# Row work of the last three stages of a graph network carried by the last 24 steps of their aggregations

## The chip, the cores and the metric

The kernel runs on 1 core of one Trainium2 chip (trn2). The metric is the time in microseconds that the device needs for one execution, as the median of several. SP, the engine without arithmetic here, issues transfers; ScalarE and GpSimd issue transfers too.

## The reference

Four layers of a graph network on 3125 nodes with 256 features and 50000 edges sorted by target node. Each layer adds its output to x; its input is relu(layernorm(x)). The first is two attention convolutions, the second adds tables, sigmoids and sums of edge attributes, the third is a convolution by relation and base, the fourth two hypergraph convolutions. What the change touches is the end of the third layer and the fourth:

```
# third: the kernel has the products with W ready in rel_d and gathers them
x = x + sum over edges of weight * (h[src] @ W[rel])
# fourth
h0 = relu((x - mean) / sqrt(var + 1e-5))                   # over features
def hconv(h, w1, b1, w2, b2, g, b):
    h = relu(h @ w1 + b1)
    agg = segment_sum(weight[:, None] * h[src], dst)
    return relu(bn(agg @ w2 + b2, g, b))                   # bn: over all nodes, with eps 1e-5
h1 = relu(bn(hconv(h0, c1...), bn1_g, bn1_b))
h2 = bn(hconv(h1, c2...), bn2_g, bn2_b)
out = x + relu(h2 + h0)
```

## The kernel before

Nodes are 25 tiles of 128 (NT), edges 196 pairs of 2 x 128 (PAIRS). An aggregation (`gather_pairs`, `act_gather_rows`, `sp_gather_rows`, `add_steps`, `multiply_steps`) walks 220 steps (T = PAIRS + NT - 1), each of one pair and one node tile: pair u and tile n meet in step u + n, so that the order works for any spread of targets, and the tile of a step is read from a table into a register. Tile n is complete for certain after step PAIRS - 1 + n.

- GpSimd (`gather_pairs`, L174 to L182) issues two indirect gathers per pair, one per half, of 128 rows of 1 KB, into a ring of 28 pairs. It waits for `slot_free`. Of the pairs in BY_ROW (every 14th from 14 to 182, 13 of them) and of the last it issues only one; the second half of a BY_ROW pair is fetched row by row, 64 rows by SP (`sp_gather_rows`, L190) and 64 by ScalarE's queue (`act_gather_rows`, L204), through `fetch_row` (L184).
- ScalarE's queue goes through all 196 pairs in order (L208 to L218): it waits until the pair three before is used up, gives the slot free, waits until the pair has landed, and raises `pair_ready` (L218); every 14 pairs it loads 14 registers (L210). It can do no arithmetic before the last pair has landed.
- VectorE (`add_steps`, L267) makes for step s two masks of 128 x 128 (L283), which hold the edge weight where an edge's target is a row of the tile, and adds the product of step s - 4 (LAG) to its tile (L299). A loop of turns of 20 steps, and four adds after it.
- TensorE (`multiply_steps`, L344) does per step two matmuls of mask by gathered rows (L374) into one of five banks (`ps`), after the mask, the pair and the add of five steps before.

`tail` (L1552) is one block of three such aggregations with what follows each. The first ("agr") sums relation rows into X. Then `dve_normalise`, `act_normalise` and `pe_normalise` take all 25 tiles: moments (L1669, L1675) in four groups, root (L1688) and reciprocal (L1661) per group, shift (L1663), normalise to HB (L1691), turn (L1707), copy (L1697 on ScalarE for 13 tiles, L1646 on VectorE for 12), product with W1 (L1636), bias (L1631), rectify (L1626, odd tiles on GpSimd at L1641), store to feat_d (L1622). For each of two convolutions (z = 0, 1) an aggregation of feat_d rows into acc follows, whose first gather waits for the stores. Then `pe_convolve`, `act_convolve` and `dve_convolve`: TensorE turns acc two tiles at a time (13 pairs, L1722), ScalarE and VectorE copy them in turn to AT (L1747), TensorE multiplies chunks of four tiles by W2 (7 chunks, L1733), ScalarE evicts to G (L1756), VectorE takes statistics (L1780), all after the last add; AT and G lie in the ring's memory, one behind the other over all tiles. `dve_coefs` (L1785 to L1794) and `act_sqrt` (L1774) make scale and shift; the norm (L1769) is run twice, and z = 0 projects with the second W1, z = 1 turns back and adds to X.

The order of an engine's instructions is written out by hand; no planner orders them. Turn buffers are four banks, two of them banks of the steps (`p_turn`), and so are those of the products (`p_proj`).

## Time and profile before

| | us |
|---|---|
| median of 3 runs | 3409.36 |
| lowest, highest | 3409.08, 3410.53 |
| span of the profiled execution | 3410.2 |
| relation aggregation, first gathers to last step | 1787 to 2266 |
| rows until the next stage's first gather | to 2307.0 |
| first convolution's aggregation | 2307 to 2788 |
| its rows | to 2859.7 |
| second convolution's aggregation | 2860 to 3342 |
| its rows and the output | to 3410.2 |

The profile gives no other time for the profiled execution than its span, 0.8 us above the median of the runs. A row of the timeline gives start, length, engine, line, operation, what it writes and reads, how many instructions are merged, and in brackets how long the engine had been idle and who ended that. A matmul of 32-bit floats is two or more passes, so a step of two matmuls shows as x4. The granted clock of TensorE is given as a share of 2.4 GHz; 0.5 is its other level, 1.2 GHz.

### The profile page before, as it was taken

Reading aid. Unit: us, or ns where it says so; the run is one execution under the profiler, and the core shown is the slowest. Engines: PE = TensorE matmul, PEld = TensorE weight load, DVE = VectorE, ACT = ScalarE, POOL = GpSimd, SP = SyncE. Lnnn points to the kernel's source line nnn. Section 1 sums busy time; section 2 is a strip of 40 time slices with the busy share of each in tenths; the row PEclk is TensorE's granted clock in tenths of the full one; section 3 lists DMA queues with packets and bytes.
Section 4 is the critical chain, followed back from the end, with each engine's and each line's share of the span. In section 5 each row is a group of like instructions: output and inputs, shape, how many; then the busy total and the mean of one; then the engine's idle time right before and its main releaser. Section 6 shows DMA issues by size and latency. Waiting matters only on the chain. (4 is left out here: it accounts for less than half of the span.)

```text
span 3410.2 us, 73948 instructions
## 1 busy us (share of the span) xinstructions
PE 2202.9 (65%) x11271; PEld 1571.4 (46%) x11272; DVE 2099.5 (62%) x5434; ACT 1368.3 (40%) x4627; POOL 2412.8 (71%) x2428
## 2 busy tenths in 40 slices
PE   5566367776665377766786666675666675666666
PEld 2355355555455265555434444453444444444443
DVE  7999877666499867766774444454444444444445
ACT  2366389998566399988670000020000013000004
POOL 5877767777777777777737777757777753777772
PEclk9789789988899789988797777787777887777787
DMA  4488734443688654443783333423333322333331
GB/s 141 120 215 229 223 101 137 137 126 104 183 230 225 198 152 145 138 121 105 208 277 110 109 109 109 125 91 107 108 108 108 109 72 87 108 109 107 109 107 55
DMA packets 347323, 465.58 MB, mean 137 GB/s; under 512 B 112217, under 2 KB 262972, under 8 KB 343812
## 3 DMA queue, kind: packets, MB, share of 16 engines
q0 software_dynamic: 111808, 284.19, 28.9%
q1 hardware_dynamic: 161972, 111.43, 11.3%
q10 hardware_dynamic: 73236, 67.28, 7.3%
q14 instruction: 288, 2.36, 0.2%
q8 instruction: 19, 0.31, 0.0%
HBM read 385.51 MB, written 76.97 MB: 136 GB/s over the span
## 5 line engine op out<-in xcount | busy, mean ns | idle before, releaser
L374 PE MATMUL t_ps<-t_ring,shared 128*128 x2640 | 920.8, 504 | 533.7 <-ACTq L218 439.8
L374 PEld LDWEIGHTS t_ps<-t_ring,shared 128*128 128x128 f32 x2640 | 611.6, 248 | 842.7 <-issue 748.2
L179 POOL DMA_INDIRECT ring<-feat_d,srcC x784 | 780.1, 995 | 253.4 <-issue 210.6
L179 POOL DMA_INDIRECT t_ring<-feat_d,srcC x756 | 725.5, 960 | 275.2 <-issue 216.6
L246 ACT ACTIVATE ring<-ring,exC 128x64 f32<-128x64 f32 x3136 | 788.2, 335 | 0.0
L374 PE MATMUL bank<-ring,arena 128*128 x1408 | 438.7, 438 | 166.6 <-ACT ring L246 129.7
L299 DVE TENSOR_TENSOR acc<-acc,t_ps 128x256 f32 x440 | 185.3, 421 | 519.6 <-PE t_ps L374 518.6
L568 POOL DMA_INDIRECT attr_d<-abuf,attr_pos x392 | 407.1, 1038 | 119.5 <-issue 119.5
L179 POOL DMA_INDIRECT t_ring<-rel_d,relC x378 | 358.6, 949 | 162.7 <-issue 106.5
L283 DVE TENSOR_SCALAR shared<-lane,dlocT,weightT 128x128 f32<-128x128 f32 x1320 | 410.0, 362 | 54.8 <-PE t_ps L374 27.5
L1747 ACT COPY t_ring<-t_pt 128x512 f32<-128x512 f32 (+1 forms) x8 | 4.2, 526 | 971.1 <-PE t_pt L1722 971.1
L374 PEld LDWEIGHTS bank<-ring,arena 128*128 128x128 f32 x1408 | 267.5, 211 | 240.0 <-issue 210.8
L969 PE MATMUL wide<-arena 128*128 128x100 bf16 x4704 | 260.5, 216 | 172.8 <-ACT arena L888 150.9
L969 PEld LDWEIGHTS wide<-arena 128*128 128x128 bf16 x4704 | 235.9, 103 | 197.8 <-DVE arena L930 106.2
L299 DVE TENSOR_TENSOR X<-X,t_ps 128x256 f32 x220 | 92.5, 420 | 251.0 <-PE t_ps L374 250.2
L299 DVE TENSOR_TENSOR acc<-acc,bank 128x261 f32 x352 | 150.3, 427 | 153.1 <-PE bank L374 146.0
L277 DVE TENSOR_TENSOR arena<-lane,dlocT 128x256 f32<-128x256 f32 x440 | 185.1, 421 | 66.9 <-issue 32.1
L884 ACT ACTIVATE arena<-arena,minus_part 128x512 bf16<-128x512 bf16 x196 | 141.4, 721 | 180.3 <-issue 114.2
L936 DVE TENSOR_TENSOR arena<-wide,shared 128x800 f32<-128x800 f32 x196 | 191.3, 976 | 8.6 <-PE wide L969 8.0
L1688 ACT ACT_TABLE_LOAD x1 | 1.3, 1283 | 485.5 <-DVE mv L1675 485.5
L945 DVE TENSOR_REDUCE shared<-arena 128x800 f32 (+1 forms) x196 | 190.4, 972 | 0.1
L364 PEld LDWEIGHTS bank<-arena 128*128 128x128 f32 x704 | 142.7, 206 | 71.8 <-issue 45.8
(307 smaller groups left out, 2615.9 us busy)
## 6 DMA issues: line engine op xcount, KB each, us to landing
arena<-lo_d ACTq DMA_DIRECT2D x392, 128.0 KB
t_ring<-feat_d SPq DMA_DIRECT2D x1664, 1.0 KB
t_ring<-feat_d ACTq DMA_DIRECT2D x1664, 1.0 KB
rel_d<-mid_stage SPq DMA_DIRECT2D x25, 1024.0 KB, 4.6
arena<-attr_d SPq DMA_DIRECT2D x98, 260.0 KB, 3.1
abuf<-in_attr SPq DMA_DIRECT2D x56, 448.0 KB
t_ring<-rel_d SPq DMA_DIRECT2D x832, 1.0 KB
t_ring<-rel_d ACTq DMA_DIRECT2D x832, 1.0 KB
```

Source lines behind the costliest of these rows:

```text
L179: pool.indirect_dma_start(out=ring[:, u % RING, j, 0:D], out_offset=None, in_=table, in_offset=bass.IndirectOffsetOnAxis(ap=index[:, u, j: ...
L246: last = act.activation(part_of_row, part_of_row, ACT.Copy, scale=exC[:, bass.ds(u, 1), j, h])
L277: last = dve.tensor_tensor(hot[:, k % NHOT, :, :], lane[:, :].unsqueeze(1).to_broadcast([P, 2, P]), dlocT[:, bass.ds(s, 1), :].rearrange(" ...
L283: last = dve.tensor_scalar(hot[:, k % NHOT, j, :], lane[:, :], dlocT[:, bass.ds(s, 1), j], weightT[:, bass.ds(s, 1), j], ALU.is_equal, ALU ...
L299: dve.tensor_tensor(acc[:, tile, 0:g.width], acc[:, tile, 0:g.width], ps[k % NHOT][:, 0:g.width], ALU.add).then_inc(g.added, 1)
L364: pe.matmul(ps_a[k % NHOT][:, 0:AW - 1], hot_a[:, k % NHOT, :], aring[:, slot, 0:AW - 1], start=True, stop=True).then_inc(g.attr_done, 1)
L374: last = pe.matmul(ps[k % NHOT][:, 0:g.width], hot[:, k % NHOT, j, :], ring[:, slot, j, 0:g.width], start=(j == 0), stop=(j == 1))
L568: pool.indirect_dma_start(out=attr_d, in_=abuf[:, g % BUFS, k, :], in_offset=None, out_offset=bass.IndirectOffsetOnAxis(ap=attr_pos[:, at ...
L884: act.activation(apart[:, k % 2, :], lo[:, k, 1, :], ACT.Abs, bias=minus_part[:, 0:1])\
L936: dve.tensor_tensor(cand[:, k % 2, :, :, :], pk[k % 2][:, :, :].rearrange("p b (s x) -> p (b s) x", x=P)[:, :, 0:HEADS * NT] .rearrange("p ...
L945: dve.tensor_reduce(e[:, bass.ds(4 * c, 4), :], cand[:, k % 2, :, :, :].rearrange("p (j q) h n -> p j h q n", q=2), AX.XY, ALU.add).then_i ...
L969: last = pe.matmul(pk[k % 2][:, j // 2, at:at + HEADS * NT], looked[:, k % 2, q, j * P:(j + 1) * P], tab[:, piece, q * HEADS * NT:(q + 1) ...
```

## The change

- `BY_ROW` ends at 168 (12 pairs). For pairs from 172 on (NOTES) `act_gather_rows` no longer runs; GpSimd raises `pair_ready` itself in `pool_note`, two pairs behind its gathers, after a wait that the pair has landed; ahead of the first such note it waits for ScalarE's 172.
- `add_steps` and `multiply_steps` take `late`, a function that is called after each step; the last two turns (40 steps) and the four adds are written out for it. From step 199 (TensorE) and 200 (VectorE) on it issues the row work tile by tile, each tile after the step that surely completes it (`wait_tile`), and what is left follows behind the last step. ScalarE runs its part (`act_rows`, `act_convolve`) freely behind pair 171.
- Relation rows: moments, root, shift per tile; all copies and rectifications on ScalarE. The root is log, then exp of minus a half, in place of sqrt and reciprocal, there and in the four coefficients of the convolutions.
- Steps have four banks, turns two of their own, W2's products one per half; G and AT are laid chunk by chunk, each in four slots of the ring.

```diff
-BY_ROW = tuple(range(ROW_STEP, PAIRS - 1, ROW_STEP))
+NOTES = 172
+PEEL = 2
+SAFE = PAIRS
+BY_ROW = tuple(range(ROW_STEP, NOTES, ROW_STEP))
...
+            if not g.gat and u - 2 >= NOTES:
+                pool_note(pool, g, u - 2)
+        if not g.gat:
+            for u in range(PAIRS - 2, PAIRS):
+                pool_note(pool, g, u)
+
+    def pool_note(pool, g, u):
+
+        if u == NOTES:
+            pool.wait_ge(g.pair_ready, NOTES)
+        pool.wait_ge(pair_landed[u % RING].sem, g.landed[u])
+        pool.sem_inc(g.pair_ready, 1)
...
-        for u in range(PAIRS):
+        for u in range(NOTES):
...
-                              ps[k % NHOT][:, 0:g.width], ALU.add).then_inc(g.added, 1)
+                              ps[k % len(ps)][:, 0:g.width], ALU.add).then_inc(g.added, 1)
...
+                if late is not None and isinstance(i, int) and i:
+                    late(s)
 
         turn(0, first=True)
-        with dve.Fori(1, T // TURN) as i:
+        ends = T // TURN - (PEEL if late is not None else 0)
+        with dve.Fori(1, ends) as i:
+            turn(i)
+        for i in range(ends, T // TURN):
             turn(i)
         dve.reg_load(regs[0:LAG], tiles[row:row + 1, T:T + LAG])
         for k in range(LAG):
             add_step(T - LAG + k, T - LAG + k, at_tile(k))
             if g.attr is not None:
                 add_attr(T - LAG + k, T - LAG + k, at_attr_tile(k))
+            if late is not None:
+                late(T + k)
...
-                pe.wait_ge(g.added, s + 1)
+                pe.wait_ge(g.added, s + 1 + NHOT - len(ps))
...
+                if late is not None and isinstance(i, int):
+                    late(s)
+
+        ends = T // TURN - (PEEL if late is not None else 0)
+        with pe.Fori(0, ends) as i:
+            turn(i)
+        for i in range(ends, T // TURN):
+            turn(i)
...
-        AT = ring_flat[:, 0:KD * NP].rearrange("p (c n) -> p c n", c=KD)
-        G = ring_flat[:, KD * NP:2 * KD * NP].rearrange("p (c n) -> p c n", c=KD)
+
+        def chunk_of(r, way):
+
+            at = 4 * D * (2 * r + way)
+            return ring_flat[:, at:at + 4 * D].rearrange("p (c m) -> p c m", c=KD)
+
+        G = [chunk_of(r, 0) for r in range(NR)]
+        AT = [chunk_of(r, 1) for r in range(NR)]
...
-        ps = [psum(f"t_ps{k}", [P, 512]) for k in range(NHOT)]
-        pt = [psum(f"t_pt0", [P, 512]), ps[4]]
+        ps = [psum(f"t_ps{k}", [P, 512]) for k in range(NHOT - 1)]
+        p_turn = [psum(f"t_pt{k}", [P, 512]) for k in range(2)]
         pf = [psum(f"t_pf{k}", [P, 512]) for k in range(2)]
-        p_turn, p_proj = pt + ps[0:2], pf + ps[2:4]
+        p_proj = [pf, pf + ps[0:2]]
...
+        def wait_tile(eng, g, n):
+
+            eng.wait_ge(g.added, NHOT + SAFE + n)
+
+        def dve_rows_late(dve, s):
+            n = s - SAFE - LAG
+            if 0 <= n < NT:
+                wait_tile(dve, g_rel, n)
+                dve.bn_stats(stats[:, n, :], X[:, n, :]).then_inc(s_stats, 1)
+            n = s - SAFE - LAG
+            if 0 <= n < NT:
+                dve.wait_ge(s_stats, n + 1)
+                dve.bn_aggr(mv[:, n, :], stats[:, n, :]).then_inc(s_var, 1)
+            n = s - SAFE - LAG - 1
+            if 0 <= n < NT:
+                dve.wait_ge(s_root, n + 1)
+                dve.scalar_tensor_tensor(out=shift[:, n:n + 1], in0=mv[:, n:n + 1, 0], scalar=-1.0,
+                                         in1=rstd[:, n:n + 1], op0=ALU.mult, op1=ALU.mult).then_inc(s_shift, 1)
+            n = s - SAFE - LAG - 5
+            if 0 <= n < NT:
+                if n == 0:
+                    dve.wait_ge(s_w, 16 * 16)
                 dve_bias(dve, 0, n)
 
...
+        def pe_rows_late(pe, s):
+            n = s - SAFE - 3
+            if 0 <= n < NT:
+                pe.wait_ge(s_norm, n + 1)
+                wait_from(pe, s_htc, n - 1)
+                for c in range(KD):
+                    last = pe.transpose(p_turn[n % 2][:, c * P:(c + 1) * P], HB[:, n, c * P:(c + 1) * P], ident[:, :])
+                last.then_inc(s_ht, 1)
+            n = s - SAFE - 5
+            if 0 <= n < NT:
+                if n == 0:
+                    pe.wait_ge(s_w, 16 * 16)
+                pe.wait_ge(s_htc, n + 1)
+                pe_project(pe, 0, n, lambda c: ht[:, n % 4, c * P:(c + 1) * P])
...
+        def act_rows(act):
+            for j in range(NT + 6):
                 if j < NT:
-                    act.wait_ge(s_shift, group_of(j) + 1)
-                    act.activation(HB[:, j, :], X[:, j, :], ACT.Relu, bias=shift[:, j:j + 1],
-                                   scale=rstd[:, j:j + 1]).then_inc(s_norm, 1)
+                    act.wait_ge(s_var, j + 1)
+                    act.activation(rstd[:, j:j + 1], mv[:, j:j + 1, 1], ACT.Ln, bias=eps[:, 0:1]).then_inc(s_log, 1)
+                n = j - 2
+                if 0 <= n < NT:
                     act.wait_ge(s_ht, n + 1)
                     wait_from(act, s_proj, n - 3)
-                    act.copy(ht[:, n % 4, :], p_turn[n % 4][:, 0:D]).then_inc(s_htc, 1)
+                    act.copy(ht[:, n % 4, :], p_turn[n % 2][:, 0:D]).then_inc(s_htc, 1)
+                if j < NT:
+                    act.wait_ge(s_log, j + 1)
+                    act.activation(rstd[:, j:j + 1], rstd[:, j:j + 1], ACT.Exp, scale=-0.5).then_inc(s_root, 1)
+                n = j - 6
+                if 0 <= n < NT:
+                    act_rectify(act, 0, n)
+                n = j - 1
+                if 0 <= n < NT:
+                    act.wait_ge(s_shift, n + 1)
+                    act.activation(HB[:, n, :], X[:, n, :], ACT.Relu, bias=shift[:, n:n + 1],
+                                   scale=rstd[:, n:n + 1]).then_inc(s_norm, 1)
...
+        def pe_convolve_late(pe, z, s):
             def turn_pair(q):
                 a0, a1 = PAIR[q]
-                if q >= 4:
-                    pe.wait_ge((s_ata, s_atd)[q % 2][z], (q - 4) // 2 + 1)
+                wait_tile(pe, g_conv[z], a1 - 1)
...
+            q, odd = divmod(s - SAFE - 3, 2)
+            if 0 <= q < NQ and not odd:
+                turn_pair(q)
+            r, rest = divmod(s - SAFE - 8, 4)
+            if 0 <= r < NR and not rest:
+                chunk(r)
...
-            for r in range(NR + 1):
-                if r >= 2:
-                    evict(r - 2)
-                if 2 * r < NQ:
-                    copy_turned(act, act.copy, z, 2 * r)
+            for r in range(NR):
+                copy_turned(act, act.copy, z, 2 * r)
+                if r >= 1:
+                    evict(r - 1)
...
-            act.activation(bsc[:, :, 0], bmv[:, :, 1], ACT.Sqrt, bias=eps[:, 1:2]).then_inc(s_sqrt[z], 1)
+            act.activation(bsc[:, :, 0], bmv[:, :, 1], ACT.Ln, bias=eps[:, 1:2]).then_inc(s_sqrt[z], 1)
+            act.wait_ge(s_sqrt[z], 2 * q + 1)
+            act.activation(bsc[:, :, 0], bsc[:, :, 0], ACT.Exp, scale=-0.5).then_inc(s_sqrt[z], 1)
...
-            dve.wait_ge(s_sqrt[z], q + 1)
-            dve.reciprocal(bsc[:, :, 0], bsc[:, :, 0])
-            dve.drain()
+            dve.wait_ge(s_sqrt[z], 2 * q + 2)
...
+        def dve_convolve_late(dve, z, s):
+            q, odd = divmod(s - SAFE - LAG - 4, 2)
+            if 0 <= q < NQ and not odd and q % 2:
+                copy_turned(dve, dve.tensor_copy, z, q)
+            r, rest = divmod(s - SAFE - LAG - 10, 4)
+            if 0 <= r < NR and not rest:
+                dve_stats(dve, s_g[z], r)
...
-                for n in range(1, NT, 2):
-                    pool_rectify(pool, n)
...
-                add_steps(dve, "agr", g_rel, hot, ps, X)
-                dve.drain()
-                dve.wait_ge(s_w, 16 * 16)
-                dve_normalise(dve)
+                add_steps(dve, "agr", g_rel, hot, ps, X, late=lambda s: dve_rows_late(dve, s))
+                for s in range(T + LAG, SAFE + LAG + 6 + NT):
+                    dve_rows_late(dve, s)
...
-                multiply_steps(pe, "agr", g_rel, ring, hot, ps)
-                pe.wait_ge(s_w, 16 * 16)
-                pe_normalise(pe)
+                multiply_steps(pe, "agr", g_rel, ring, hot, ps, late=lambda s: pe_rows_late(pe, s))
+                for s in range(T, SAFE + 5 + NT):
+                    pe_rows_late(pe, s)
                 for z, tag in enumerate(convs):
-                    multiply_steps(pe, f"ag{tag}", g_conv[z], ring, hot, ps)
-                    pe_convolve(pe, z)
+                    multiply_steps(pe, f"ag{tag}", g_conv[z], ring, hot, ps, late=lambda s: pe_convolve_late(pe, z, s))
+                    for s in range(T, SAFE + 5 + 4 * NR):
+                        pe_convolve_late(pe, z, s)
```

## Rows read from the trace of the kernel before

**Rows 1.** The page, part 4: the chain that ended last, shares of the span by line

```profile
POOL t_ring L179 20%; ACTq L187 5%; DMA t_ring<-feat_d,srcC 2%; ACTq L227 2%; ACTq L210 1%; DMA t_ring<-rel_d,relC 1%; PE t_ps L374 1%; PE t_pf L1636 1%; PE t_pf L1733 1%; PE t_ps L1733 1%; PE t_ps L1636 1%; DVE t_bn L1780 1%; DMA t_ring<-feat_d 0%; DMA t_ring<-rel_d 0%; PE t_ps L1722 0%
```

**Rows 2.** Windows: length, busy PE, PEld, DVE, ACT, POOL, granted clock, DMA share, GB/s

```profile
2307.00:2788.00 481.00, 306.70 (x880) 204.61 (x880) 204.74 (x652) 0.00 (x0) 362.90 (x378) 0.76 0.37 107
2788.00:2860.00 72.00, 51.88 (x208) 35.89 (x206) 36.37 (x80) 40.94 (x76) 5.76 (x2) 0.88 0.13 46
```

**Rows 3.** Waits of GpSimd from 1780 us on (total, times, longest), then timeline around 2261 to 2307

```profile
POOL t_ring L179 <- issue: 323.1, 1059, 0.3
...
2261.09 0.95 POOL L179 DMA_INDIRECT t_ring<-rel_d,relC  x1 [0.30 <-issue]
...
2303.94 0.42 ACT L1626 ACTIVATE shared<-shared 128x256 f32<-128x256 f32 x1 [1.31 <-DVE shared L1631]
...
2306.99 1.12 POOL L179 DMA_INDIRECT t_ring<-feat_d,srcC  x1 [3.02 <-DMA feat_d<-shared]
```

**Rows 4.** ScalarE's notes from 2209 to 2263 us: ns shortest/median/longest, first and last start

```profile
L218 ACTq EVENT_SEMAPHORE  x24: 17/17/38, 2209.3 to 2262.6; - x24
```

**Rows 5.** Chain at the end of relations: from the second-last gather's start to its landing

```profile
2259.83 2.74 DMA t_ring<-rel_d,relC
```

**Rows 6.** Timeline of TensorE, last steps of relations

```profile
2222.80 2.07 PE L374 MATMUL t_ps<-t_ring,shared 128*128 x4 [0.69 <-DVE X L299]
...
2236.58 7.21 PE L374 MATMUL t_ps<-t_ring,shared 128*128 x24 [4.05 <-ACTq L218]
```

**Rows 7.** Groups by line and shape, 2263 to 2310: count, busy us, mean ns, idle before

```profile
L1691 ACT ACTIVATE HB<-X,shift,rstd 128x256 f32<-128x256 f32 x25 | 14.3, 592 | 0.5 <-DVE shift L1663 0.5
L1626 ACT ACTIVATE shared<-shared 128x256 f32<-128x256 f32 x13 | 5.4, 417 | 8.1 <-DVE shared L1631 8.1
L1697 ACT COPY shared<-t_ps 128x256 f32<-128x256 f32 x9 | 3.2, 357 | 0.0
...
L1669 DVE BATCH_NORM_STATS2 stats<-X 128x6 f32<-128x256 f32 x25 | 8.9, 414 | 0.1
L1631 DVE TENSOR_TENSOR shared<-t_pf,t_b 128x256 f32<-128x256 f32 x13 | 5.5, 422 | 3.5 <-PE t_pf L1636 3.5
...
L1675 DVE BATCH_NORM_AGGREGATE mv<-stats 128x2 f32<-128x6 f32 x25 | 2.1, 154 | 0.3
L1663 DVE SCALAR_TENSOR_TENSOR shift<-mv,rstd 128x2 f32<-128x2 f32 x1 | 0.2, 161 | 0.1
```

**Rows 8.** Timeline of VectorE in the last steps of relations: masks and an add

```profile
2255.36 0.60 DVE L283 TENSOR_SCALAR shared<-lane,dlocT,weightT 128x128 f32<-128x128 f32 x2
...
2257.19 0.42 DVE L299 TENSOR_TENSOR X<-X,t_ps 128x256 f32 x1 [1.23 <-PE t_ps L374]
```

**Rows 9.** Timeline of TensorE in the row work: two turns in a row, a projection between

```profile
2296.14 0.38 PE L1707 MATMUL t_pt<-ident,HB 128*128 128x128 f32 x2
...
2297.22 0.38 PE L1707 MATMUL t_ps<-ident,HB 128*128 128x128 f32 x2
```

**Rows 10.** First convolution: last step, a turn and a chunk in the chain, a statistic, the aggregation

```profile
2787.16 1.13 PE L374 MATMUL t_ps<-t_ring,shared 128*128 x4 [0.38 <-ACTq L218]
...
2794.98 0.44 PE t_ps L1722 x4
2795.42 3.44 PE t_ps L1733 x8
...
2814.48 0.69 DVE L1780 BATCH_NORM_STATS2 t_bn<-t_ring 128x6 f32<-128x512 f32 x1 [1.25 <-ACT t_ring L1756]
...
2817.20 0.55 DVE L1785 BATCH_NORM_AGGREGATE t_bmv<-t_bn 128x2 f32<-128x42 f32 x2
```

**Rows 11.** ScalarE by line, 1200 to 1800: log, exp and table load of the stage before

```profile
L1431 ACT ACTIVATE mid_root<-mid_moments,mid_eps 128x2 f32<-128x2 f32 x27 | 7.8, 289 | 0.0
L1439 ACT ACTIVATE mid_root<-mid_root 128x2 f32<-128x2 f32 x27 | 5.3, 195 | 0.1
...
L1417 ACT ACT_TABLE_LOAD x1 | 1.3, 1283 | 6.0 <-PEq L103 6.0
```

More of the change, by code:

```diff
@@ L353, in multiply_steps, with turn @@
             pe.sem_inc(g.attr_added, NHOT)
-        with pe.Fori(0, T // TURN) as i:
+        def turn(i):
             pe.reg_load(regs, slots[row:row + 1, bass.ds(TURN * i, TURN)])
@@ L1867, in _ @@
                 act.wait_ge(s_eps, 1)
[L1868 removed]
+                act_rows(act)
                 for z, tag in enumerate(convs):
```

133 lines of the change are left out of this document (32 added, 101 removed).

## The prediction

> **What bounds the kernel now.** I began with the page: the chain that ended last is led by GpSimd's (POOL's) gathers at L179, 20% of the span, and no other line has more than 5% [rows 1]. The windows by stage show two kinds of stretch: long aggregations (relations, then two convolutions), in which ScalarE does no arithmetic at all and GpSimd is the busiest, and gaps between them, in which GpSimd is nearly idle and TensorE, VectorE and ScalarE do the row work [rows 2]. Inside an aggregation the waits of GpSimd are almost all "issue", 0.3 us before each gather and never more [rows 3]: a gather is 0.95 us and 0.30 us of issue, 1.25 us, back to back, 378 to a stage. So each aggregation lasts as long as GpSimd's queue, and nothing on the other engines lengthens it. After the last gather the row work stands bare: relations issue the last gather at 2261.09 and the next stage's first one starts at 2306.99 [rows 3]; the first convolution's last step starts at 2787.16 and the aggregation of its statistics, with which the coefficients begin, at 2817.20 [rows 10]. These are the stretches that the change can shorten.
>
> **Part 1, a gather more and the notes of GpSimd.** BY_ROW loses pair 182, so GpSimd issues its second half itself: one gather, 1.25 us per stage [rows 3]. ScalarE and SP lose 64 row fetches each, which nothing waited for except TensorE (its 4.05 us stall near the end, ahead of a burst of six steps, belongs to pair 182 and ScalarE's register load there [rows 6]; it goes). The 24 late pairs are noted by GpSimd: a wait and an increment each, on the queue that sets the stage. No row shows them on that queue. Below: on ScalarE's queue such an instruction takes 17 ns [rows 4], two are 0.034 us, 0.8 us per stage. Above: a full issue gap of 0.30 us each [rows 3], 7.2 us. I take 0.05 us, near ScalarE's row because it is the same kind of instruction: 1.2 us per stage. The waits themselves should find their pair landed: a pair is noted 2.8 us after its last gather began (2.74 us of transfer, then the note) [rows 5], and GpSimd asks only after two more pairs, 6.0 us after that start. The first late note also waits for ScalarE's 172 notes; the last of these came at 2209.3 [rows 4], while GpSimd would ask at about 2211.8 (seven pairs of 2.5 us before pair 181's end). Slack 2.5 us, so nothing. TensorE sees late pairs 6.0 - 2.8 = some 3.3 us later than now, but the last two at once when landed. Sum on GpSimd's queue: +2.5 us per stage.
>
> **Part 2, relations.** The late work starts with VectorE's iteration of step 200. Counted back from the last, step 199 is the TensorE row at 2222.80 [rows 6]; step 196 ends about 2218, with the 3.3 us of part 1 2221.5. Per iteration VectorE does two masks in 0.60, an add in 0.42 [rows 8], row statistics 0.41, aggregation 0.15, shift 0.16, bias 0.42 [rows 7]: 2.2 us, with four more waits about 2.4. ScalarE does log 0.29, exp 0.20 [rows 11], copy 0.36, rectify 0.42, normalise 0.59 [rows 7]: 1.9, with waits 2.1 to 2.3. TensorE does a step of some 0.9 when queued (1.13 with its latency [rows 10]) and a turn with a projection at 1.09 [rows 9]: 2.0. Steps come every 2.25 us (18 pairs for 20 steps). So VectorE is the slowest, and only slightly: iterations 200 to 204 without bias, five at 1.9, then fifteen at 2.4, end at 2267; 220 to 223 have no masks, four at 1.75, 2274; tile 24 has its moments at 2275.5. Then one tile passes log, exp, shift, normalise, turn, copy, projection, bias and rectify behind ScalarE's older tiles: about 6 us, 2281.5. From the end of the last rectification to the first gather it was 2.6 us [rows 3] and stays so: 2284. The queue's 2.5 us are mostly covered by VectorE's own pace; I add 1. **2285 for 2307: -22 us.** The table load ahead of the roots (1.28 us) goes with it, and so do the 12 rectifications of GpSimd.
>
> **Part 3, each convolution.** Step 219 began at 2787.16 [rows 10]. Turning, W2 and eviction took from its end, 2788.3, to the coefficients at 2817.2: 28.9 us, in which TensorE is busy nearly throughout, a chunk being 3.44 us [rows 10]. Now four of seven chunks and eleven of thirteen turns lie inside the steps. There TensorE needs, for four steps, 4 x 0.9 + 3.44 + 2 x 0.44 = 7.9 us against 9 us of gathers: it fits. At the end it doesn't quite: pair 192 is noted at 2783.7, its step and chunk 3 hold TensorE until 2788.1, then three steps and two turns, 2791.7. Left are chunk 4 (3.44), two turns (0.65), a copy (0.8), chunk 5 (3.44), chunk 6 (about 1.0), and 0.9 for eviction and statistics: 2802.1. With +2.5 of the queue 2804.6 for 2817.2: **-12.6 us each.** Log and exp in place of root, reciprocal and drain are 0.5 us against 0.57: nothing. Four step banks for five: TensorE then waits for an add that VectorE makes four steps behind, 0.42 us, while TensorE idles 1 to 3 us per step waiting for notes; that idling hides it. Single banks for W2 wait for an eviction of four steps before, hidden likewise. Unrolled turns issue the same instructions as the loop: nothing, and up to 3 us per stage if straight code is slow to arrive.
>
> **Sum.** -22 - 12.6 - 12.6 = -47 us. On the profiled span of 3410.2 that is 3363; the median of the runs is 3409.36, 0.8 below the span, so I predict 3362.5. What a measurement of this kernel can tell from no change is about 0.2%, 7 us.
>
> **A rule against the row.** Gathers issued beside VectorE's masks keep their 0.95 us and 0.30 us; the longest here is 1.12, with the masks of the first steps just before it [rows 3]. The Trainium skill (SBUF — State Buffer, the part on engine ports) says that VectorE in a two-port mode locks GpSimd out of a shared port pair, so that its DMA descriptors wait until VectorE is done. The rule would make the masks, which are here already, a visible cost, and the rows don't show it; so the sum takes no lengthening from the added VectorE work.
>
> **Rivals.**
> (a) *Late work falls behind the steps.* All three engines are within 15% of the pace and wait for each other in order; TensorE's next step is queued behind a turn that waits for ScalarE. If an iteration is 3.2 us rather than 2.4, relations end at 2221.5 + 24 x 3.2 + 9 = 2307, gain nothing, and the convolutions gain 9 each: 3391. A step at the low clock is 2.07 us against 1.13 [rows 6, 10]; over 21 steps that is 20 us, the upper bound for TensorE. For: the mean clock in the steps is 0.76 against 0.88 between stages [rows 2]. Against: it is lower where TensorE idles, and it will idle less.
> (b) *VectorE's added work holds the gathers.* If each added statistic (0.41, 20 times in relations; 0.69, six times in each convolution) held GpSimd for its length: 8 + 4 + 4 us, 3379. The masks speak against it.
> (c) *Slower: tables switch between log and exp.* If the two were in different tables, each tile in relations would load twice, 2 x 1.28 us [rows 11], an iteration of ScalarE 4.7 us, 26 of them 122 us from 2221.5 on, and 6 to the gather: 2350, +43; the convolutions would keep 8 each: 3437. It decides from an iteration of 3.3 us on. Against: the stage before uses both functions, 27 exps of that kind, with one load [rows 11].
> (d) *Slower: GpSimd's notes stall its queue.* If the wait drained the queue, or landing took over 6 us rather than 2.8, a note would cost a gather slot: 24 x 1.25 x 3 = 90 us, 3452. From 0.7 us per note on it eats the gain.
>
> **Chances.** Forecast and its neighbourhood (notes 0.03 to 0.3, iterations of 2.2 to 2.7): 0.68. (a) 0.17, of which 0.03 within 0.2% of before. (b) 0.06. (c) 0.03. (d) 0.04. Unnamed 0.02, in the range. Low end: notes at 0.03 and iterations at the bare 2.2 gain 5 more in relations, and TensorE's queue at the end of a convolution 3 more each: 3351. High end: notes at 0.3 cost 6 x 3 = 18, or (b), or most of (a): 3385. Faster 0.90, same 0.03, slower 0.07.
>
> **What would show it.** Right: GpSimd's first gather of the first convolution 20 to 24 us sooner after the relation gathers' end; no ACT_TABLE_LOAD in the tail; first coefficients about 16 us (not 30) behind the last step's old place; ScalarE with arithmetic inside the last 50 us of relations; late gathers at 1.25 to 1.30 us of distance. Wrong: gaps of over 0.5 us between gathers of pairs 174 to 195 (d); loads between L1431-like logs and exps (c); steps 200 to 219 over 2.7 us apart (a). A stretch between aggregations that is unchanged would refute parts 2 and 3.

## The result, and the profile after

The kernel after took 3335.89 us (median of 4 runs, 3333.11 to 3338.23) beside 3409.95 for the kernel before (4 runs, 3409.08 to 3411.67): a ratio of 0.9785 [0.9772, 0.9797], 74 us less. The prediction had 3362.5 (3349 to 3386), so the sign was right and the gain was put 27 us too small, outside the range. The profiled span fell from 3410.2 to 3331.4, by 78.8. A later comparison of the same two kernels, told below, gave 68 us less in place of 74.

Where the 78.8 us lie is read from GpSimd's gathers, by the start of the first and the end of the last of each row. The forecast's -22 and -12.6 hold the queue's +2.5, which has rows of its own here:

| stretch | before | after | difference | forecast |
|---|---|---|---|---|
| start to the first relation gather | 1788.4 | 1777.5 | -10.9 | 0 |
| relation gathers (378, now 379) | 473.6 | 474.9 | +1.3 | +2.5 |
| behind them, to the first of convolution 1 | 44.95 | 18.2 | -26.7 | -24.5 |
| gathers of convolution 1 | 477.9 | 474.75 | -3.2 | +2.5 |
| behind them | 74.75 | 56.5 | -18.3 | -15.1 |
| gathers of convolution 2 | 477.65 | 475.0 | -2.7 | +2.5 |
| behind them, to the end | 72.9 | 54.5 | -18.4 | -15.1 |

The relation stage's end in the trace after, GpSimd's timeline (start, length, engine, line, operation, names, count, idle before it and what ended that):

```profile
2250.24 0.94 POOL L181 DMA_INDIRECT t_ring<-rel_d,relC  x1 [0.30 <-issue]
2251.49 0.95 POOL L181 DMA_INDIRECT t_ring<-rel_d,relC  x1 [0.30 <-issue]
2270.66 0.98 POOL L181 DMA_INDIRECT t_ring<-feat_d,srcC  x1 [18.23 <-DMA feat_d<-shared]
```

These answer to [rows 3]: the gap was 45 us and is 18.2, and the distances at the stage's end are still 1.25. Before that end, TensorE's timeline shows a step (L395), a turn (L1705) and a projection (L1671) in turn, here a tile in 2.04 us:

```profile
2225.76 1.13 PE L395 MATMUL t_ps<-t_ring,shared 128*128 x4 [0.44 <-POOLq L196]
2226.72 0.38 PE L1705 MATMUL t_pt<-ident,HB 128*128 128x128 f32 x2
2226.94 1.03 PE L1671 MATMUL t_pf<-shared 128*128 128x256 f32 x4
2227.80 1.03 PE L395 MATMUL t_ps<-t_ring,shared 128*128 x4
```

VectorE's timeline of the same stretch shows who sets that pace:

```profile
2229.95 0.42 DVE L1666 TENSOR_TENSOR shared<-t_pf,t_b 128x256 f32<-128x256 f32 x1
2230.29 0.59 DVE L297 TENSOR_SCALAR shared<-lane,dlocT,weightT 128x128 f32<-128x128 f32 x2
2230.92 0.42 DVE L313 TENSOR_TENSOR X<-X,t_ps 128x256 f32 x1
2231.26 0.42 DVE L1683 BATCH_NORM_STATS2 stats<-X 128x6 f32<-128x256 f32 x1
2231.72 0.18 DVE L1687 BATCH_NORM_AGGREGATE mv<-stats 128x2 f32<-128x6 f32 x1
2231.82 0.13 DVE L1691 SCALAR_TENSOR_TENSOR shift<-mv,rstd 128x1 f32<-128x1 f32 x1
2231.90 0.42 DVE L1666 TENSOR_TENSOR shared<-t_pf,t_b 128x256 f32<-128x256 f32 x1
```

A tile's seven instructions sum to 2.16 us by their lengths, as the prediction added them up, but the next tile's bias starts 1.95 us after this one's: at four of the joins an instruction begins 0.05 to 0.08 us before the one ahead of it is over. VectorE is back to back in such a stretch. Over the whole window it is not, as the view by windows has it (busy us of PE, PEld, DVE, ACT and POOL, then TensorE's granted clock, the DMA share and GB/s):

```profile
2225.00:2250.00 25.00, 22.16 (x110) 18.11 (x109) 20.40 (x77) 15.68 (x54) 19.02 (x20) 1.00 0.54 157
```

20 gathers in 25 us: GpSimd still sets the pace, and the other three keep to it. The last tile's moments end at 2259.42, 7.0 us behind the last gather, and its rectification at 2268.14, 8.7 us after them:

```profile
2259.24 0.18 DVE L1687 BATCH_NORM_AGGREGATE mv<-stats 128x2 f32<-128x6 f32 x1
...
2267.72 0.42 ACT L1661 ACTIVATE shared<-shared 128x256 f32<-128x256 f32 x1 [0.45 <-DVE shared L1666]
```

GpSimd's notes, as the trace has line 196:

```profile
L196 POOLq EVENT_SEMAPHORE  x72: 17/17/2587, 2195.3 to 3279.0; - x72
  PE t_ps L395: 24.4, 26
```

(shortest, median and longest in ns; then who waited). The median is 17 ns, as on ScalarE [rows 4]. The longest, 2.59 us, is the first note of the stage: it stands until its pair has landed, and no gather behind it came late. TensorE waits for the notes 24.4 us in all, 26 times. Where a note lies among the gathers shows for pair 192 of the first convolution. Its second gather is the first row here; its note (a row of the view of line 196) is out before the two gathers of pair 194, which stand ahead of it in the program:

```profile
2738.19 0.95 POOL L181 DMA_INDIRECT t_ring<-feat_d,srcC  x1 [0.30 <-issue]
...
L196 POOLq EVENT_SEMAPHORE  x1: 17/17/17, 2740.9 to 2740.9; - x1
...
2741.94 0.95 POOL L181 DMA_INDIRECT t_ring<-feat_d,srcC  x1 [0.30 <-issue]
2743.19 0.96 POOL L181 DMA_INDIRECT t_ring<-feat_d,srcC  x1 [0.30 <-issue]
```

The end of the first convolution:

```profile
2742.48 3.60 PE L1756 MATMUL t_pf<-t_ring,shared 128*128 128x512 f32 x8
...
2744.46 0.95 POOL L181 DMA_INDIRECT t_ring<-feat_d,srcC  x1 [0.30 <-issue]
...
2745.91 1.03 PE L395 MATMUL t_ps<-t_ring,shared 128*128 x4
...
2747.21 1.89 PE L395 MATMUL t_ps<-t_ring,shared 128*128 x8
...
2749.51 3.67 PE L1756 MATMUL t_pf<-t_ring,shared 128*128 128x512 f32 x8
...
2754.45 4.12 PE L1756 MATMUL t_pf<-t_ring,shared 128*128 128x512 f32 x12 [0.61 <-ACT t_ring L1770]
...
2758.90 0.71 PE L1756 MATMUL t_pf<-t_ring,shared 128*128 128x128 f32 x4 [0.33 <-ACT t_ring L1779]
...
2760.35 0.55 DVE L1809 BATCH_NORM_AGGREGATE t_bmv<-t_bn 128x2 f32<-128x42 f32 x2
```

It answers to [rows 10]. The last gather ends at 2745.41 and the coefficients begin 14.9 us later; it was 32.3 (2784.93 to 2817.20), forecast 17.2. TensorE comes out of chunk 3 at about 2746.0, 0.6 us behind the last gather (forecast 3.2), runs the last three steps and two turns, and then chunks 4, 5 and 6 take 10.8 us to the coefficients (forecast 10.4). From there to the next stage's first gather it is 41.6 us, and was 42.5.

Last, the page's costliest GpSimd groups, of the kernel before and of the one after, in that order:

```profile
L179 POOL DMA_INDIRECT ring<-feat_d,srcC x784 | 780.1, 995 | 253.4 <-issue 210.6
L179 POOL DMA_INDIRECT t_ring<-feat_d,srcC x756 | 725.5, 960 | 275.2 <-issue 216.6
L568 POOL DMA_INDIRECT attr_d<-abuf,attr_pos x392 | 407.1, 1038 | 119.5 <-issue 119.5
L179 POOL DMA_INDIRECT t_ring<-rel_d,relC x378 | 358.6, 949 | 162.7 <-issue 106.5
```

```profile
L181 POOL DMA_INDIRECT ring<-feat_d,srcC x784 | 772.9, 986 | 252.8 <-issue 217.8
L181 POOL DMA_INDIRECT t_ring<-feat_d,srcC x758 | 719.2, 949 | 291.4 <-issue 215.4
L597 POOL DMA_INDIRECT attr_d<-abuf,attr_pos x392 | 403.0, 1028 | 119.4 <-issue 119.4
L181 POOL DMA_INDIRECT t_ring<-rel_d,relC x379 | 359.6, 949 | 163.3 <-issue 108.0
```

A gather from feat_d took 960 ns and takes 949; one from rel_d took 949 in both. That is 0.011 us for each of some 380 gathers a stage, 4 us, and the earlier stages, which the change leaves alone, are shorter by 10.9 us together. Their 784 gathers are 9 ns shorter each and their 392 scatters (attr_d) 10 ns, 11 us by length and some 9 by the distances of their starts. No step of the prediction speaks of it.

### The profile page after: what moved, and what is told of

It reads as the page before. It is cut to its first block and busy times, and to the rows that moved or that the text cites. A ratio compares the mean times of both kernels' runs of the same rounds, so it can differ in the third digit from the quotient of the medians.

```text
span 3331.4 us, 73355 instructions
## 1 busy us (share of the span) xinstructions
PE 2175.0 (65%) x11271; PEld 1559.5 (47%) x11272; DVE 2091.5 (63%) x5435; ACT 1383.2 (42%) x4700; POOL 2386.6 (72%) x2419
## 5 line engine op out<-in xcount | busy, mean ns | idle before, releaser
L395 PE MATMUL t_ps<-t_ring,shared 128*128 x2640 | 905.8, 496 | 492.7 <-ACTq L232 393.8
L395 PEld LDWEIGHTS t_ps<-t_ring,shared 128*128 128x128 f32 x2640 | 602.7, 245 | 790.7 <-issue 702.1
L395 PE MATMUL bank<-ring,arena 128*128 x1408 | 429.3, 431 | 165.0 <-ACT ring L260 126.6
L395 PEld LDWEIGHTS bank<-ring,arena 128*128 128x128 f32 x1408 | 261.0, 206 | 237.6 <-issue 210.9
L1718 ACT ACTIVATE rstd<-mv,t_eps 128x1 f32<-128x1 f32 x25 | 7.2, 286 | 437.6 <-DVE mv L1687 437.6
```

What stands on the lines that cost most here:

```text
L395: last = pe.matmul(ps[k % len(ps)][:, 0:g.width], hot[:, k % NHOT, j, :], ring[:, slot, j, 0:g.width], start=(j == 0), stop=(j == 1))
```

## Is it the carrying? One part alone

Some runs come from chips on which both kernels take some 4820 us; they are told further down. Those here took the ordinary time.

**Nothing carried, all else kept.** The row work runs behind the steps again, with the notes, one gather more, buffers by chunk, logarithms, four banks and ScalarE's rectifications as after.

```diff
-                add_steps(dve, "agr", g_rel, hot, ps, X, late=lambda s: dve_rows_late(dve, s))
-                for s in range(T + LAG, SAFE + LAG + 6 + NT):
+                add_steps(dve, "agr", g_rel, hot, ps, X)
+                for s in range(SAFE + LAG, SAFE + LAG + 6 + NT):
```

and likewise on TensorE and for the convolutions.

> The same kernel as the run before it of that name (no row work carried, everything else of the change kept), asked for again because in that call the straight code of ScalarE's and SP's queues was held up and set the time. If GpSimd's gathers set the stages again (before at about 3410): theory (the tails' gain of 63 us comes from the carrying): tails of 45, 75 and 73 us or a little more, 3399 to 3415. Rival (much comes from the other edits): 35, 65 and 63 or less, 3370. If the queues are held up again: 1% above before, as measured there (4869 for 4820), and the first case stays open.

Measured: 3419.96 us, 1.0011 [1.0002, 1.0021] of the kernel before; the unchanged after beside it,

> The changed kernel again. If gathers set the stages: distance of the feat_d gathers 1.253 us and 3333 to 3338 us if it belongs to the kernel; anywhere from 1.250 to 1.265 and up to 3355 us if it is a matter of loading. In the call where the queues were held up its distance was 1.254 and that of the kernel before 1.261, which speaks for the kernel.

took 3345.58, 0.9787 [0.9771, 0.9803]. That is 68 us under the 3413.95 of the kernel before and 7.6 us above what was expected; in its profile the relation gathers begin at 1786.2 where the first profile of the kernel has 1777.5 (before: 1788.4), and the convolutions' are 1.2567 and 1.2565 us apart. So outside the edited stretches this profile is some 8 us shorter than that of the kernel before, where the first one is 19 us shorter by the same terms. The stretches behind the gathers are 56.4, 79.8 and 76.6 us without carrying and 17.6, 57.5 and 54.3 with it: 83.5 us less. Nothing carried, the time is 5 us over the most that was expected. So carrying brings the whole gain in the edited stretches, and the edits that make it possible cost some 11, 5 and 4 us behind the three stages when nothing is carried (against 44.95, 74.75, 72.9).

**The notes alone**, with the gather that comes with them, in the kernel before (first late note at pair 172, BY_ROW up to 168, nothing else).

```diff
+            if not g.gat and u - 2 >= NOTES:
+                pool_note(pool, g, u - 2)
```

> The same kernel as the run before it of that name (only the notes of the late pairs moved to GpSimd). If gathers set the stages: notes free and gather distance unchanged (1.264 us for feat_d): each row of gathers one gather longer, 3412 to 3415. Rival (notes or ScalarE's shorter queue speed up the gathers): feat_d gathers at 1.253, 3390 to 3400.

Measured: 3419.49 us beside a before of 3413.95, 1.0016 [1.0006, 1.0026]; 4.5 us over the range that was given, and the kernel before stood 4 us higher too. The relation row is 475.25 us for 379 gathers; 378 of before's distances (1.2538) and a gather are 474.9, which is what the kernel after took. So 24 notes cost between nothing and 0.4 us, and the gather its 1.25.

**Nine increments for one.** A late note is followed by eight more (increments of a semaphore that nobody waits for), 192 a stage.

```diff
+        for _ in range(8):
+            pool.sem_inc(g.spare, 1)
```

> The changed kernel with eight more increments of an unused semaphore behind each of GpSimd's late notes, 24 x 8 = 192 more such instructions per stage. Theory (such instructions are hidden, as the queue runs ahead of the gathers): every row of gathers stays 474.7 to 476.7 us, 3332 to 3347 us. Rival (0.05 us each on the path, as my prediction took): 9.6 us per stage, 3361 to 3375.

Measured: 3336.47 us, distances 1.2540, 1.2531, 1.2532 as after. No cost of theirs shows: they lie beside the gathers' own time.

**A note right behind its pair.** GpSimd asks for pair u after issuing it, not after pair u + 2.

```diff
-            if not g.gat and u - 2 >= NOTES:
-                pool_note(pool, g, u - 2)
+            if not g.gat and u - 0 >= NOTES:
+                pool_note(pool, g, u - 0)
```

> The changed kernel, but GpSimd notes a late pair directly behind that pair's own gathers, not two pairs later. In the changed kernel pair 192 is noted 2.7 us after its second gather starts, which is before the gathers that stand ahead of the note in the program have started: so GpSimd's queue runs ahead of its gathers. Theory (the wait for landing holds the queue, and with no gathers queued behind it GpSimd stands still until 2.75 us after the start of the pair's last gather): a late pair takes 1.25 + 2.75 = 4.0 us and some 0.3 of issue for two gathers instead of 2.5, 24 x 1.8 = 43 us per stage, 3 x 43 = 130 us less what the row work, better hidden then, gives back (5 to 10 a stage): 3440 to 3465 us. Rival (a wait does not hold the gathers behind it): 3332 to 3347.

Measured: 3508.42 us. The wait does hold the queue, as GpSimd's timeline near the relation stage's end shows:

```profile
2271.89 0.95 POOL L181 DMA_INDIRECT t_ring<-rel_d,relC  x1 [0.30 <-issue]
2275.41 0.95 POOL L181 DMA_INDIRECT t_ring<-rel_d,relC  x1 [2.57 <-DMA t_ring<-rel_d,relC]
2276.67 0.94 POOL L181 DMA_INDIRECT t_ring<-rel_d,relC  x1 [0.30 <-issue]
2280.16 0.95 POOL L181 DMA_INDIRECT t_ring<-rel_d,relC  x1 [2.55 <-DMA t_ring<-rel_d,relC]
```

72 notes cost some 172 us, 2.4 each, where 1.8 was expected and 3440 to 3465 us in all. This is rival (d), one argument away from the kernel that was timed: the two pairs between gather and note are what makes the notes free. A distance of one pair was not tried.

## The smaller parts

**Root and reciprocal for logarithm and exponential**, in the kernel after (the drain between reciprocal and shift comes back).

```diff
-                    act.activation(rstd[:, j:j + 1], mv[:, j:j + 1, 1], ACT.Ln, bias=eps[:, 0:1]).then_inc(s_log, 1)
+                    act.activation(rstd[:, j:j + 1], mv[:, j:j + 1, 1], ACT.Sqrt, bias=eps[:, 0:1]).then_inc(s_root, 1)
```

> The changed kernel with sqrt and reciprocal for every root. Theory (that edit is worth nothing here): one table load inside the relation steps, VectorE 0.17 us and a drain more per tile, ScalarE an exp of 0.2 less per tile; relation tail 18 us within 1.5, convolutions within 0.5, time 3336 to 3349 as the changed kernel's. Rival (ScalarE's log and exp are what bounds the late rows): relation tail 16 us or less. Theory L on the gather distance: 1.265 us, 3353 to 3365.

Measured: 3331.77 us, 0.9771 [0.9755, 0.9787]: the interval holds the after's 0.9785. No worth of log and exp shows here, as forecast. The other way round, **log and exp in the kernel before**,

> The kernel before with log and exp for the roots (four groups, and the four coefficients), no reciprocals, no drains behind them. Theory L (the gather distance goes with this edit, in some way that I can't name): 1.254 to 1.257 us, 3388 to 3396. Else 1.265; and the table load of 1.28 us goes from the relation rows: 1 to 2 us faster than before, 3408 to 3418.

took 3415.07 us in one execution beside 3409.59, its stretch behind the relations 44.35 us against 44.95. Its three rows of gathers are 4 us longer than in the first profile of the kernel before, which the edit doesn't explain.

**GpSimd rectifies the odd tiles again**, in the kernel after.

```diff
+                for n in range(1, NT, 2):
+                    pool.wait_ge(s_bias, n + 1)
+                    pool.tensor_scalar(stage[:, n % 5, :], stage[:, n % 5, :], 0.0, None, ALU.max).then_inc(s_relu_odd, 1)
```

> The changed kernel, but GpSimd rectifies the odd tiles of the relation rows again, behind its gathers. Theory P: feat_d gathers 1.265 us apart, 3353 to 3365 us. Else 1.254 to 1.257. The rectifications themselves: GpSimd takes them up only behind its last gather and note, so the stages of twelve tiles free late; five stage buffers hold up bias and projection, and TensorE's and VectorE's steps with them: relation tail 5 to 10 us longer than 18.

Measured: 3375.76 us in one execution, above the 3353 to 3365 expected, and 40.2 us behind the relation gathers, where after has 18.2 and 23 to 28 was expected. GpSimd's timeline, and a row of VectorE's, show why:

```profile
2263.19 0.95 POOL L181 DMA_INDIRECT t_ring<-rel_d,relC  x1 [0.30 <-issue]
2266.25 2.49 POOL L1882 TENSOR_SCALAR shared<-shared 128x256 f32<-128x256 f32 x3 [2.11 <-DMA t_ring<-rel_d,relC]
...
2268.94 0.42 DVE L1670 TENSOR_TENSOR shared<-t_pf,t_b 128x256 f32<-128x256 f32 x1 [25.14 <-DMA feat_d<-shared]
...
2271.22 0.87 POOL L1882 TENSOR_SCALAR shared<-shared 128x256 f32<-128x256 f32 x1 [2.48 <-DVE shared L1670]
...
2304.35 1.13 POOL L181 DMA_INDIRECT t_ring<-feat_d,srcC  x1 [3.00 <-DMA feat_d<-shared]
```

The first rectification stands behind the last gather in GpSimd's queue and behind the last notes. The seventh tile's bias needs the stage buffer that the second tile still holds, so VectorE, with its masks and adds queued behind that bias, stands for 25.14 us until 2268.94; only six biases came before. Of the 26.7 us won behind the relations, 22 hang on this move to ScalarE. The rest of the longer time lies in the gathers, 1.2663 and 1.2646 us apart in the convolutions, and ahead of the relations, whose first gather is at 1789.6.

**And in the kernel before**, ScalarE rectifies all tiles:

> The kernel before, but ScalarE rectifies the odd tiles of the relation rows too, so that GpSimd has no arithmetic of its own between its gathers there. Asked: what makes the feat_d gathers 1.265 us apart in the kernel before and 1.254 to 1.257 in the changed one, in every stage from the first. Theory P (it goes with GpSimd's program having that arithmetic instruction): 1.254 to 1.257 us here, 3388 to 3396 us. Else 1.265 and 3409 to 3420.

Measured: 3400.41 us (one execution) beside 3409.59, but behind the relations 43.85 us, only a microsecond less; the rest are gathers: their distance in the convolutions fell from 1.265 to 1.2566 and 1.2563, and the relations begin at 1783.2 in place of 1788.4.

**A denser set of row pairs** (ROW_STEP 12 for 14, so 14 pairs up to 168 have a half brought row by row).

> The changed kernel with every 12th pair fetched half by row instead of every 14th (ROW_STEP = 12, 14 pairs instead of 12), so two gathers fewer for GpSimd in each of the three stages. Theory (GpSimd's row of gathers sets the stages): 2 x 1.25 x 3 = 7.5 us faster than the changed kernel, 3325 to 3338. Rival (SP needs 0.475 us per row, 30.4 us for its 64, as long as the gathers of 12 pairs; it falls behind and slots come late): same or slower, up to 3360.

Measured: 3448.45 us, 1.0107 [1.009, 1.0124]: far above both the theory and its rival. GpSimd's waits show why:

```profile
POOL t_ring L181 <- POOLq L196: 116.6, 3, 40.0
```

Three times, once a stage, GpSimd stood some 39 us before pair 175. The note of pair 172 stands right ahead of it and waits for ScalarE's 172 notes, and these for pair 168, the last with rows. In the relation stage SP had its 64 rows of that pair issued at 2201.1, ScalarE only at 2237.9; its 172nd note came at 2241.1 and the gather at 2242.0. Issuing 64 rows takes ScalarE 26 to 30 us there, and the 23 gathers of twelve pairs take 28.8, so it falls behind; in the kernel after, with the 33.8 us of fourteen pairs, its 172nd note is at 2195.3, right behind the gathers of pair 172. In the kernel before no gather stands behind ScalarE's note of a pair, only behind a slot that it gives free; after, pair 175 does.

## A chip on which the change does not pay

> The kernel before, unchanged, as a second profile of it. What is asked: the gathers of feat_d start 1.264 us apart in the first profile of the kernel before and 1.253 in that of the changed kernel, in stages that the change doesn't touch too. Theory A (the distance is a matter of the loading of a program or of the moment, not of the change): this profile shows another distance than 1.264, anywhere between 1.250 and 1.265, and the time is 3390 to 3410 us by it (about 1550 gathers and 392 scatters at 0.01 us each are 20 us). Theory B (it belongs to the kernel): 1.264 again and 3408 to 3412 us.

> The changed kernel, unchanged, as a second profile of it. Theory A (loading or moment): the distance of the feat_d gathers may come out anywhere from 1.250 to 1.265 us, the stages before the relations' first gather take 1777 to 1789 us, the time is 3333 to 3355 us. Theory B (it belongs to the kernel): 1.253 us again, the relations' first gather at 1777 to 1779, 3333 to 3338 us.

> The kernel before with only the late pairs' notes moved to GpSimd (NOTES = 172, BY_ROW to 168, GpSimd's own waits and increments); all row work stays behind the last step. Theory A (notes cost nothing, gather speed does not depend on them): each aggregation's row of gathers is one gather (1.25 us) longer and the stretch behind it the same within 1 us, 3 to 5 us slower than before: 3412 to 3415. Rival (GpSimd's notes or ScalarE's shorter queue speed up the gathers): feat_d gathers at 1.253 us, 3390 to 3400. Rival (the notes cost what my prediction took, 0.05 us each): 3417.

> The changed kernel, but no row work carried by the steps: the late functions all run behind the last step, in the same order, and the turns stay a loop. Everything else of the change stays (notes, ScalarE for all copies and rectifications, log and exp, four step banks, two turn banks). Theory (the tails' gain of 63 us comes from the carrying): the stretches from the last gather of a stage to the first of the next go back to 45, 75 and 73 us or a little more, since two turn banks and ScalarE's larger share slow the row work: 3335.9 + 63 = 3399, up to 3415. Rival (much of the gain comes from the other edits): stretches of 35, 65 and 63 or less, 3370.

These ran on one chip. Measured, beside a before of 4819.82 us (18 runs): before again 4814.64, 0.9994 [0.9979, 1.0008]; after 4840.62, 1.005 [1.0031, 1.007]; notes alone 4846.88, 1.0057 [1.0038, 1.0077]; nothing carried 4869.09, 1.0112 [1.0074, 1.0149]. GpSimd's longest waits, of after and then of before:

```profile
POOL ring L181 <- ACTq L253: 799.7, 144, 267.5
POOL t_ring L181 <- ACTq L227: 419.4, 174, 5.9
...
POOL t_ring L181 <- POOLq L196: 131.2, 3, 44.9
```

```profile
POOL ring L179 <- ACTq L239: 791.9, 147, 267.6
POOL t_ring L179 <- ACTq L213: 469.6, 196, 7.5
```

There GpSimd waits for ScalarE's releases of slots in either kernel. In the relation stage of the kernel before SP's 64 row fetches take 35 to 42 us from the second row pair on, where the ordinary profile has 23.3, and the gathers of fourteen pairs take 33.8; from the start of one of SP's fetches to the next it is 0.7 to 3 us 284 times, where the ordinary profile has that 15 times. Why the fetches run late on that chip was not found. Carrying still wins, 28 us against nothing carried, but the kernel with the notes alone is 27 us slower than the kernel before, of which 4 were expected: it has three waits of 43 us each at the note's line, as in the run with the denser rows. The prediction gave that wait a slack of 2.5 us and priced it at nothing; that holds only where the fetches keep up.

## The gathers that came closer together

The 0.011 us was followed through the runs. Kernels in which GpSimd rectifies (before, notes alone, before with log and exp, after with GpSimd's rectifications) have 1.263 to 1.269 us in the convolutions on the chips of the ordinary kind; those in which it doesn't (after, its variants but the two whose gathers were held, and before with ScalarE's) have 1.253 to 1.257. Two single edits show it from both sides: taking the rectifications off GpSimd in the kernel before brings the distance down by 0.008 to 0.009, and giving them back to it in the kernel after brings it up by 0.010 to 0.013 (one execution each). Theory: arithmetic on GpSimd slows the gathers behind it. **One such instruction at the very end** of the kernel after, on a spare tile,

> The changed kernel and, behind the last gather of all, one GpSimd tensor_scalar on a tile of 128 x 2 (after a memset that it waits for); nothing else. Theory P (the presence of that kind of instruction anywhere in GpSimd's program slows the gathers of feat_d and the scatters by 0.008 to 0.012 us each from the first one on): feat_d gathers 1.264 to 1.268 us apart, 3350 to 3362 us. Rival (it is the length or place of the code, or the twelve instructions between the stages): 1.253 to 1.257 us, 3332 to 3347.

left 3335.23 us and 1.2539, 1.2536, 1.2540. **Twelve, between relations and the first convolution**, then **twelve at the end**, and **an unused DRAM buffer ahead of feat_d** in the kernel before:

> The kernel after, with a GpSimd memset and twelve GpSimd tensor_scalar instructions on a spare 128x2 tile, depending on nothing else, between the relation gathers and the first convolution's. Where the question is why gathers of feat_d are 0.011 us further apart in kernels in which GpSimd rectifies. If having done such instructions just before slows the gathers that follow: relations stay at 1.254 us, both convolutions go to 1.265 (+4 us each), about 3345. If it is the dependence on VectorE's and SP's tiles, or chance of placement: all three stages stay at 1.254 and the time is 3337 to 3342 (twelve short instructions lie in a stretch in which GpSimd waits anyway).

> The same memset and twelve instructions behind the last gather of the program instead. If doing them before the gathers is what slows them, nothing is slower: distances 1.254 in all three stages, 3335 to 3340. If the number of such instructions in the program counts wherever they stand, the convolutions go to 1.265 here too and the feature stage's median to 1.26.

> The kernel before with one more, unused, internal buffer of 128x256 in DRAM declared ahead of feat_d, so that feat_d and rel_d may lie elsewhere. If the slow gathers are a matter of where feat_d lies, the distance of the convolutions' gathers may fall from 1.265 to 1.254 and the time by about 8 to 12 us, to 3398 to 3402 beside a before of 3410; if not, 1.265 and the same time as before.

These three ran on another chip, with times like those of the chip of the late fetches (4839.95, 4854.82 and 4813.62 us beside 4821.2), so their times say little, but the gathers that follow each other unhindered can still be compared. The mean distance of those under 1.35 us apart in the convolutions is 1.2540 and 1.2542 for the two with twelve instructions, 1.2540 for the kernel after, 1.2608 for before with the buffer and 1.2611 for before. So neither the instructions, nor their place, nor that buffer moves it (where the table came to lie was not seen). What is left is something that goes with the real rectifications (the tiles they write, their waits and their semaphore) or with the program's layout. It stays open. The distance also moves by 0.003 us between profiles of one kernel (1.2567 and 1.2534 in the first convolution of after, with 1786.2 and 1777.5 us ahead of the relations), so some 10 us of the profiled difference are no more certain than that.

## Why the prediction was right, and where it failed

The mechanism was right and the sum too small: 47 us were forecast, 74 came. **The step that failed is the sum itself.** It adds the three edited stretches and the queue's own gather and notes, and so puts everything else, the stages ahead of the relations and the distance of the gathers, at nothing. Measured in its place: -10.9, -4.4 and -4.0 us, 19 of the 32 us between forecast and profiled difference. Two smaller terms were mis-sized with it, in parts 1 and 2; with these alone the forecast would have come out at some 3350, inside its range.

*The bound.* Right. Gathers at some 1.25 us before and after; most of the gain lies behind them, -26.7, -18.3 and -18.4, in sum -63.4 of -78.8, and that part vanishes when nothing is carried.

*Part 2, the relations.* Right: -26.7 for a forecast of -24.5 against the last gather. VectorE is the slowest, as forecast, at 1.95 us a tile where 2.2 was summed and 2.4 taken: the lengths of neighbouring instructions overlap, and the four more waits show as no more than 0.04 us twice. So it could catch up with the gathers' 2.25: the last tile's moments came 7.0 us behind the last gather, where the forecast has 11 and another 1 for the queue. The way of that tile to its rectification took 8.7 us, not 6, and gave 2.7 of these 5 back. The 2.2 us by which the stretch came out shorter are these two, so that it came out so near is in part luck. That GpSimd's rectifications "go with it" was true and was the least weighed sentence: put back, they take 22 of those 26.7 us.

*Part 3, the convolutions.* The mechanism was right, the size wrong. The term behind it is the last but one sentence on part 1, that TensorE sees late pairs some 3.3 us later than now. The prediction let GpSimd ask only when the gathers of two more pairs are over. In the trace after, pair 192's note, whose second gather began at 2738.19, is at 2740.9, at its landing 2.7 us later and ahead of the gathers of pair 194 at 2741.94 and 2743.19, which stand before it in the program; all 24 notes of that stage are over 2.7 to 2.9 us after their pair's last gather began. The queue behaves as if it had taken those gathers in already and ran ahead of what it shows as busy. So chunk 3 held TensorE until 0.6 us behind the last gather and not 3.2. That is 2.6 of the 3.2 us by which the first convolution came out shorter; the last chunks gave 0.4 back, and 0.9 lie behind the coefficients.

*Part 1, the price of a note.* 0.05 us was taken, with 0.034 and 0.3 as bounds. No price shows: one gather explains the relation row's +1.3, and nine increments for one changed no distance. The queue costs 3.8 us over the three stages, not 7.5. The same running ahead would explain a price below the lower bound.

*The slack of 2.5 us of the first late note.* Enough where the kernel was timed: ScalarE's 172nd note is at 2195.3, and pair 175's first gather, the first that this wait could hold, starts at 2201.4. Where the row fetches are late the wait costs 37 to 45 us a stage.

*Left out altogether.* Of the 32 us between forecast and profiled difference, 19 (10.9 before the relations, 4.4 and 4.0 in the convolutions) go with gathers and scatters that came closer together; in the second profile of the kernel after it is some 8. The edit that moves the distance is the one of the rectifications, by the two runs that change it alone; by what mechanism is open, and no row of the kernel before could have shown it. The stretches behind the gathers make 8.7 and the queue 3.7 of the rest. The range had no term on its lower side for anything outside the edited stretches.

*The rivals.* (a) Late work kept up. (b) Gathers beside VectorE's added statistics keep 1.25. The Trainium skill's rule on engine ports (SBUF — State Buffer) has VectorE lock GpSimd out while it runs in a two-port mode. The prediction took the masks for such instructions. No row here tells in which mode an instruction ran, so the rule itself is not tested; what is measured is that with VectorE busy for 20.4 of 25 us 20 gathers took 19.02 us, 0.951 each. (c) No load between logarithms and exponentials, and roots instead of them time alike. (d) True of a note right behind its pair, false of one two pairs later. Log and exp were priced at nothing, and nothing showed. Four banks and unrolled turns, priced likewise, were not tried singly; together with the rest of the scaffolding they cost up to 11, 5 and 4 us when nothing is carried.

## What to carry to other kernels

When one engine's queue sets a stage's length, the next stage's row work can be hung on the steps of the stage before, at the slower of the pace and the busiest helper's sum per tile; here the sum of the lengths in the group rows was above what the helper took (2.16 us for 1.95). The instructions of the carried chain have to leave the pacing queue: half the rectifications left there gave 22 of 27 us back. A wait on the pacing queue was free two pairs behind its cause and cost 2.4 us right behind it, and it ties that queue to whatever the wait counts.

## What the hardware showed that was not expected

- GpSimd's queue runs ahead of its gathers: notes are out 2.7 us after a gather began although two gathers ahead of them in the program have not begun, 72 notes and 576 further increments show no cost, and yet a wait right behind its pair stops the gathers for 2.57 us.
- VectorE's short instructions overlap: seven of 2.16 us in sum follow each other in 1.95.
- The same gathers of feat_d take some 949 or 960 ns by the program, and those of rel_d 949 in both, already in stages before the difference; moving twelve rectifications between GpSimd and ScalarE moves it both ways, while twelve spare GpSimd instructions and a buffer ahead of the table don't.
- Two chips ran either kernel at some 4820 us instead of 3410; on the one where both were timed, GpSimd waited over 1200 us for ScalarE and the kernel after was 0.5% slower.
